# A three-layer graph attention stack on one core: chunk 0's sums during the count stage, 40 count tiles, and the maxima of five chunks over four chunks of products

## The reference, cut to what matters

```
h = x @ W
s = h @ a_src ; d = h @ a_dst
e = leaky_relu(s[src] + d[dst], 0.2)
m = segment_max(e, dst)
ex = exp(e - m[dst])
z = segment_sum(ex, dst)
out = segment_sum((ex / z[dst])[:, None] * h[src], dst) + b
```

## Time and profile before

| | |
|---|---|
| median of 3 runs | 714.85 us (714.55 to 715.75) |
| profiled execution | 714.44 us, its span 712.6 us |
| VectorE busy | 674.7 us (95%) |
| TensorE busy, its weight loads | 604.9 us (85%), 588.5 us (83%) |
| ScalarE busy | 463.8 us (65%) |
| GpSimd busy | 368.3 us (52%) |
| mean granted TensorE clock | 0.934 |
| chain that ended last | VectorE 56%, TensorE 30%, issue 9% |

### The profile page before, as it was taken

The page is one execution under the profiler, slowest core; times in us unless marked ns, Lnnn a source line. Parts: engine busy times, 40 slices in busy tenths (PEclk is TensorE's granted clock), DMA queues, the critical chain, the costliest instruction groups (busy, mean ns, idle before and its releaser), DMA issues.

```text
span 712.6 us, 13778 instructions
## 1 busy us (share of the span) xinstructions
PE 604.9 (85%) x5576; PEld 588.5 (83%) x5576; DVE 674.7 (95%) x939; ACT 463.8 (65%) x696; POOL 368.3 (52%) x354
## 2 busy tenths in 40 slices
PE   2657677675589899999999979999989889999995
PEld 1557666665589899999998979898979889999995
DVE  3999999999999999999999799999999989999995
ACT  0326666454497557575666768878776698687780
POOL 5581000000045454454675666758588677696883
PEclk9956889677789999999999999999999999999998
DMA  3410000001000000000100100000010010100001
GB/s 76 112 47 1 2 1 1 1 8 3 35 1 20 1 18 1 19 1 1 9 36 2 26 2 18 1 19 1 2 10 36 1 27 1 36 17 22 19 1 41
DMA packets 22325, 12.07 MB, mean 17 GB/s; under 512 B 12393, under 2 KB 20055, under 8 KB 22255
## 3 DMA queue, kind: packets, MB, share of 16 engines
q1 hardware_dynamic: 21455, 9.85, 5.9%
q0 software_dynamic: 800, 1.26, 0.6%
HBM read 9.47 MB, written 1.64 MB: 16 GB/s over the span
## 4 chain that ended last, share of the span: by engine, by line
DVE 56%; PE 30%; issue 9%; POOL 3%; ACT 1%; DMA 1%; DVEq 0%; POOLq 0%
PE ps L1739 23%; DVE scratch L864 22%; DVE ps L980 15%; DVE scratch L1062 9%; DVE ps L982 2%; DVE ps L992 2%; PE ps L1792 2%; PE ps L1695 1%; PE ps L1770 1%; POOL scratch L673 1%; DVE scratch L980 1%; DMA gathered<-in_edges,start_i 1%; DVE bn L814 1%; PE ps L1762 1%; PE ps L1795 0%
## 5 line engine op out<-in xcount | busy, mean ns | idle before, releaser
L1739 PE MATMUL ps<-hB,scratch 125*125 125x129 f32 x3450 | 404.2, 276 | 23.9 <-DVE scratch L1062 20.3
L1739 PEld LDWEIGHTS ps<-hB,scratch 125*125 125x125 f32 x3450 | 390.8, 189 | 32.2 <-DVE scratch L1062 24.5
L673 POOL TENSOR_TENSOR scratch<-scratch,C 125x625 f32<-125x625 f32 x197 | 250.8, 1284 | 178.9 <-ACT scratch L1500 178.9
L980 DVE SCALAR_TENSOR_TENSOR ps<-C,a_unit,ps 125x625 f32<-125x625 fp8e3 x330 | 278.0, 868 | 2.3
L1498 ACT ACTIVATE scratch<-gathered,r_neg 125x625 f32<-125x625 f32 x197 | 159.3, 809 | 43.1 <-PE ps L1739 40.9
L1500 ACT ACTIVATE scratch<-scratch,r_src 125x625 f32<-125x625 f32 x197 | 160.9, 817 | 6.4
L1062 DVE SCALAR_TENSOR_TENSOR scratch<-ps,r_src,C 125x625 f32<-125x625 f32 x178 | 153.5, 862 | 5.7 <-PE ps L1729 5.7
L1695 PE MATMUL ps<-scratch 128*128 128x125 bf16 x1250 | 105.9, 260 | 49.5 <-DVE scratch L864 49.5
L1695 PEld LDWEIGHTS ps<-scratch 128*128 128x128 bf16 x1250 | 99.8, 120 | 55.4 <-DVE scratch L864 54.1
L1363 ACT ACTIVATE C<-ps 125x1500 fp8e3<-125x1500 f32 (+2 forms) x60 | 75.3, 1270 | 73.8 <-PE ps L1695 73.5
L864 DVE TENSOR_TENSOR scratch<-key_lo,ps 128x5376 bf16<-128x5376 bf16 (+3 forms) x31 | 87.8, 2833 | 0.2 <-PE ps L1695 0.2
(11 more groups left out here) (185 smaller groups left out, 419.4 us busy)
## 6 DMA issues: line engine op xcount, KB each, us to landing
gathered<-g_lines SPq DMA_DIRECT2D x15, 305.2 KB
xr<-in_x SPq DMA_DIRECT2D x1, 1562.5 KB
out<-xr SPq DMA_DIRECT2D x4, 312.5 KB
edge_sb<-in_edges SPq DMA_DIRECT2D x1, 805.7 KB
gathered<-ext_lines SPq DMA_DIRECT2D x5, 122.1 KB
w<-in_W SPq DMA_DIRECT2D x2, 128.0 KB
out<-xr SPq DMA_DIRECT2D x1, 187.5 KB
out<-xr SPq DMA_DIRECT2D x1, 125.0 KB
```

The lines of the kernel that those rows point to most:

```text
L673: g.tensor_tensor(slot[s], slot[s], C5[:, q % NC, s, :], ALU.mult).then_inc(pool_done, 1)
L980: v.scalar_tensor_tensor(dest, counts, unit[:, s:s + 1], top, ALU.min, ALU.max).then_inc(S.top_done, 1)
L1739: last = mm(ps[0:P, acc_at(t):acc_at(t) + HW], A[:, P * t:P * (t + 1)], feat, start=opens and t in (0, 3), stop=closes, skip_group_check=True)
```

## The change

1. `SPLIT` cuts a chunk's windows into 8 tiles of up to 16, so there are 40 count tiles. This makes the one-hot buffers small enough that the ring of eight block buffers stands beside them in `scratch` (the ninth lies in `gathered`). The two halves of a tile are 8 and 8 windows.
2. The keys of chunks 1 to 4 are transposed at tiles 5 to 8, and the seven attention rounds stand at tiles 9 to 15. The extremes, scalars and exponentials follow at 16, 18 and 19.
3. All 25 blocks of chunk 0 are made by ScalarE and GpSimd within the count tiles 21 to 39 (`EARLY`), one or two a tile, and TensorE adds them two tiles later (`LAG`). GpSimd also scales the first layer's features (`scale_tiles`, five instructions of 645 columns, in place of 25 on ScalarE).
4. VectorE has no chunk 0 any more. Behind the first five maxima it goes on with the chunks of products 1 to 4, and the maxima of chunks 0 to 4 are spread over them (`FIRST_TOPS`). In chunks 1, 2 and 3 VectorE makes 5, 11 and 9 products (`OWN`); ScalarE and GpSimd make 20, 14 and 16. Chunk 4 and all later ones are as before.
5. What turns sums into the next features (`FIRST_LAYER`) stands later in chunks 1 to 3, in part in the chunk behind.

```diff
@@ -48,10 +48,10 @@
     assert EX % U == 0 and WC == P
-    SPLIT = (0, 21, 42, 63, 84, 105, P)
+    SPLIT = (0, 16, 32, 48, 64, 80, 96, 112, P)
...
     NT = NC * JT
-    WMAX = 21
+    WMAX = 16
@@ -178,9 +178,10 @@
-        ring = [scratch[0:P, i * CD:(i + 1) * CD] for i in range(RING + 1)]
+        ring = [scratch[0:P, 2 * OH + i * CD:2 * OH + (i + 1) * CD] for i in range(RING)]
+        ring.append(gathered[:, :, :].rearrange("p g e -> p (g e)").bitcast(fp32)[:, 1500:1500 + CD])
         slot = [ring[s % RING if s < T - 1 else RING] for s in range(T)]
-        at = (RING + 1) * CD
+        at = 0
@@ -228,12 +229,12 @@
                 ps[0:P, NEW + 512:NEW + 512 + 2 * AW].rearrange("p (t f) -> p t f", f=AW)]
-        PREP, VEC, CNT, COV = 2560, 2048, 3584, 3648
-        DIF, KEYS0, KEYS_AT = 3072, (0, 512), (3584, 3584 + KC * P)
+        PREP, VEC, CNT, COV = 1024, 2048, 3584, 3648
+        DIF, KEYS0, KEYS_AT = 2560, (0, 512), (3584, 3584 + KC * P)
         G0T, AB0 = 3584, 3584 + 4 * P
-        HALF = [(0, 12, 0), (12, WMAX, 2048)]
+        HALF = [(0, 8, 1024), (8, WMAX, 2048)]
         LAST_AT = 3072
-        IOTA = 1536
+        IOTA = 3072
@@ -361,11 +362,15 @@
         FEATS = tuple((t, min(t + 4, T)) for t in range(0, T, 4))
-        FEAT_AT = (5, 7, 9, 11, 13, 15, 17)
         KEYS_TILE = 4
-        EXT_AT, OVER_AT, EXPS_AT = 20, 23, 24
-        SCALED_AT = 26
-        SCALED = tuple(range(2, 10)) + (0, 1) + tuple(range(10, T))
+        FEAT_AT = tuple(KEYS_TILE + WG + r for r in range(len(FEATS)))
+        EXT_AT = FEAT_AT[-1] + 1
+        OVER_AT = EXT_AT + 2
+        EXPS_AT = OVER_AT + 1
+        EARLY_AT = EXPS_AT + 2
+        LAG = 2
+        EARLY = {t: tuple(range((t - EARLY_AT) * T // (NT - EARLY_AT), (t + 1 - EARLY_AT) * T // (NT - EARLY_AT)))
+                 for t in range(EARLY_AT, NT)}
@@ -376,6 +381,10 @@
                    At(1, (3, 4, 5, 6), 6, (8, 9, 10), None, (14, 17, 20), (None,) * 3, (None,) * 3, None, None))
+        FIRST_LAYER = (None,
+                       At(14, (15, 15, 16, 16), 16, (17, 17, 18), None, (23,), (21, 23, 27), (23, 25, 29), 25, 27),
+                       At(10, (11, 11, 12, 12), 12, (13, 13, 14), None, (20,), (17, 20, 25), (19, 22, 27), 22, 24),
+                       At(4, (5, 5, 6, 6), 6, (7, 7, 8), None, (16,), (13, 16, 22), (15, 18, 24), 19, 21))
@@ -392,7 +401,20 @@
+        OWN = ((), (15, 17, 19, 21, 23), (1, 4, 6, 8, 10, 12, 14, 16, 18, 20, 22), (1, 4, 7, 10, 13, 16, 18, 20, 22))
+        def spread_tops(q, k0, k1, s0, s1):
+            return tuple((s0 + (k - k0) * (s1 - s0) // (k1 - k0), q, k) for k in range(k0, k1))
+        AFTER = T
+        FIRST_TOPS = (None,
+                      spread_tops(0, AHEAD, T, 0, 13) + spread_tops(1, 0, 10, 14, 25) + spread_tops(1, 10, 14, AFTER, AFTER),
+                      spread_tops(1, 14, T, 0, 10) + spread_tops(2, 0, 17, 10, 25) + spread_tops(2, 17, 21, AFTER, AFTER),
+                      spread_tops(2, 21, T, 0, 4) + spread_tops(3, 0, T, 4, 24) + spread_tops(4, 0, AHEAD, AFTER, AFTER))
         def pool_tiles(q):
+            if q < len(OWN):
+                return tuple(s for s in range(T) if s not in OWN[q])
@@ -404,12 +426,22 @@
             L = (q - 1) // NC
+            if q < len(FIRST_LAYER):
+                return FIRST_LAYER[q]
...
-        def in_odd(k):
+        def in_odd(k, q=None):
+            if q in (1, 2):
+                return k % 2 == 1 and not any(at_ == AFTER and (c, k) == (q, k_) for at_, c, k_ in FIRST_TOPS[q])
...
         LAST_ODD = max(k for k in range(T) if in_odd(k))
+        def tops_before_rows(q):
+            if q in (2, 3):
+                c, k = min((c, k) for at_, c, k in FIRST_TOPS[q - 1] if at_ == AFTER)
+                return c * (T + 1) + k
+            return q * (T + 1) if q > 1 else 0
@@ -703,8 +735,12 @@
                 t1 = t0 + CT
-                pool.wait_ge(exps_ready, EXPS[L, 0 if t0 < EARLY_TILES else t0])
-                pool.wait_ge(F.pe_done, (L * NC - 1) * T + t1)
+                pool.wait_ge(exps_ready, EXPS[L, 0 if L == 0 or t0 < EARLY_TILES else t0])
+                if L:
+                    pool.wait_ge(F.pe_done, (L * NC - 1) * T + t1)
+                else:
+                    pool.wait_ge(keys_sb, 2 * WG)
+                    pool.wait_ge(h_ones, 1)
@@ -748,12 +784,17 @@
                             scale_tiles(L, LATE)
-                    if q < NC and s in B2_AT:
+                    if q == 0 and s % CT == 0:
+                        scale_tiles(0, s)
+                    if 0 < q < NC and s in B2_AT:
...
                         block_product(q, s)
+                if q == 0:
+                    for t in range(CT):
+                        second_bias(t)
@@ -1075,12 +1123,15 @@
                     elif s == 0:
-                        dve.wait_ge(F.rows_ready, q + 1)
-                    for k in range(AHEAD, T):
-                        if top_at(q, k) == s:
-                            next_top(q, k)
-                    if s == join_at(q):
-                        join_tops(F, q)
+                        dve.wait_ge(F.rows_ready, q)
+                    if q < len(FIRST_TOPS):
+                        first_tops(q, s)
+                    else:
+                        for k in range(AHEAD, T):
+                            if top_at(q, k) == s:
+                                next_top(q, k)
+                        if s == join_at(q):
+                            join_tops(F, q)
@@ -1153,7 +1205,7 @@
                 next_top(0, k)
-            for q in range(Q):
+            for q in range(1, Q):
@@ -1499,17 +1531,39 @@
+            def count_stage():
+                for t in range(NT):
+                    if 0 < t - KEYS_TILE < WG:
+                        copy_keys(t - KEYS_TILE)
+                    if t + 1 in FEAT_AT:
+                        normalise_first(FEAT_AT.index(t + 1))
+                    if t in FEAT_AT:
+                        features_out(FEAT_AT.index(t))
+                    if t == EXPS_AT:
+                        act.wait_ge(sig_ready, 1)
+                        exps_dst(0, 0, T)
+                        exps_src(0, 0, T)
+                        first_negative_r()
+                    counts_out(t, 0)
+                    if t in FEAT_AT:
+                        attention_out(FEAT_AT.index(t))
+                    for p in EARLY.get(t, ())[:1]:
+                        row_maximum(0, p)
+                    counts_out(t, 1)
+                    for p in EARLY.get(t, ())[1:]:
+                        row_maximum(0, p)
...
                 for s in range(T):
-                    if q == 0 and s + 10 < T:
-                        scale_features(SCALED[s + 10])
...
                         after_sums(F, q - 1, post_at(q), s)
+                    if 1 < q <= len(FIRST_LAYER):
+                        after_sums(F, q - 2, post_at(q - 1), s + T)
@@ -1529,15 +1583,13 @@
+            count_stage()
...
             act.wait_ge(half_out[1], NT + 1)
-            for s in SCALED[8:10]:
-                scale_features(s)
-            act.wait_ge(rneg_ready, 1)
-            for p in POOL_OF[0]:
-                if pass_at(0, p) < 0:
-                    row_maximum(0, p)
-            for q in range(Q):
+            for p in POOL_OF[1]:
+                if pass_at(1, p) < T:
+                    row_maximum(1, p)
+            for q in range(1, Q):
@@ -1721,11 +1759,11 @@
                     pe.wait_ge(g_done, LINES[L, EARLY_TILES])
-                if q:
+                if q > 1:
...
                 for t in range(CT):
-                    if t == CT - 1 and q:
-                        pe.wait_ge(F.top_done, q * (T + 1))
+                    if t == CT - 1 and q > 1:
+                        pe.wait_ge(F.top_done, tops_before_rows(q))
@@ -1806,6 +1844,31 @@
+            def first_block(s):
+                pe.wait_ge(pool_done, s + 1)
+                if s % CT == 0:
+                    pe.wait_ge(y_scaled, s // CT + 1)
+                if s < T - 2:
+                    products(slot[s], hB3[:, s, :], F.pe_done, s == 0, False)
+                elif s == T - 1:
+                    last_products(0)
+            def count_stage():
+                pe.wait_ge(keys_sb, 2)
+                for t in range(NT):
+                    if t == KEYS_TILE:
+                        sum_covered()
+                    if 0 < t - KEYS_TILE < WG:
+                        transpose_keys(t - KEYS_TILE)
+                    if t in FEAT_AT:
+                        features(FEAT_AT.index(t))
+                    count(t, t == NT - 1)
+                    for s in EARLY.get(t - LAG, ()):
+                        first_block(s)
+                for t in range(NT - LAG, NT):
+                    for s in EARLY[t]:
+                        first_block(s)
@@ -1813,10 +1876,8 @@
                         pe.wait_ge(prod_done, prod_no(q, s) + 1)
-                    if q == 0:
```

(5 more changed lines are left out.)

75 lines of the change are left out of this document (27 added, 48 removed).

## The result

The changed kernel took 710.65 us (median of four, 708.67 to 712.06) beside 715.11 for the kernel before: ratio 0.9935, 95% interval 0.991 to 0.9961. The gain is 4.5 us; the forecast had 11.2. The profiled execution was the fastest of the four, 708.67 us with a span of 706.9, which is 5.7 less than the span of before. So part of the miss lies in the profile (5.5 us: 708.67 for 703.2) and part in the distance from it to the median (2.0 us, where 0.4 was allowed).

The account below looks back on a forecast made before the run. VectorE bounds the count stage; TensorE, with VectorE 1.2 us behind, the first layer's steady chunk. Z to chunk 5 shrinks 17.0 us, less 5.8 for Z moving: 11.2 off 714.44 is 703.2, plus 0.4 gives 703.6 us, range 692.5 to 712.

Parts of the forecast that it names:

- Z: Start of the first maximum, after the count stage: 198.35 us in before, forecast to move by 5.8 us.
- (b)1: Hand-over after Z: rows wait for chunk 0's last two blocks, arriving at Z+10.7; VectorE idles 6.3 us.
- (b)3: Chunk 1: transposes follow TensorE's block 14, so VectorE idles 5.7 us before L1033 and ends at Z+49.4.
- (b)2: Start of chunk 1: ScalarE makes six row blocks before copying sums; TensorE starts at Z+16.3, losing 1.7 us to its clock.
- (b)4: Chunks 2 and 3: VectorE binds with 43 big instructions each, 37.0 and 36.2 us; TensorE needs 34.2 at most.
- (b)5: Chunk 4: its 0.82 us of idle time goes, 35.5 becomes 34.7 us; chunk 5 starts at Z+157.3.
- (a)3: Attention rounds on tiles 9 to 15: chain of 5.1 to 6.7 us against VectorE's 4.4; stall 2 to 8, taken 3.
- (a)1: Count stage: 40 tiles for 30 give 20 more compare instructions at 0.06 us each, +1.2 us.
- (a)2: Count stage: node statistics, now behind four smaller tiles, wait for x to land, +0.8 us.
- (a)4: Count tiles from 21: 25 blocks on 19 tiles fit under 4.4 us on average; +0.8 us, bounds 0 and 3.
- ScalarE and TensorE pace the early blocks: Rival, count stage: rounds at half clock add 5 us, early tiles at mean clock 0.77 add 2.2: 711, chance 0.12.
- The product work wasn't the limit: Rival, first layer's products: maxima, 125 as before, and stalls eat the whole gain: 714.9, chance 0.04.

Follow-up runs that it names:

- e1_after: The changed kernel run again with no edit, beside the kernel before: 711.08 us, ratio 0.9953.
- e9_rows: Changed kernel with TensorE's row broadcast for chunk 1 called ahead of the last products of chunk 0: 710.4 us, ratio 0.9946.
- e2_pool: Changed kernel with three products each of chunks 2 and 3 moved from VectorE to ScalarE and GpSimd: 705.97 us, ratio 0.9885.
- e12_terms: Changed kernel with attention products behind their tile's count products, and ScalarE's copy of their results behind its half 1 copy: 706.7 us, ratio 0.9874.
- e6_spread: Changed kernel with attention rounds on tiles 9, 10, 12, 13, 15, 16, 18 and early blocks from tile 24: 709.95 us, ratio 0.9927.
- e14_all: Changed kernel with e12_terms' order, e2_pool's products, and rows, sums copy, transposes and kappa exponential earlier around chunk 1: 700.71 us, ratio 0.9795.

## Why the prediction was right in sign and wrong in size

The miss is 7.0 us (710.65 for 703.6). On the forecast's own clock it is 1.0 before Z, -0.3 to the end of chunk 1, 4.6 in chunks 2 to 4, 0.2 behind, and 1.6 between the profile and the median. None of the three signs of being wrong that the prediction names came: the clock after tile 21 was 0.91, a 4096-element compare took 2.28 us, and ScalarE had copied half 0 of the last tile at Z+1.7 (forecast Z+2.6). Of what it says would show it, two things failed: chunk 5 came 161.6 us after Z and not some 157, and VectorE idled in chunk 3.

**What bounds the kernel, (b)1 to (b)3: right.** Both engines lost work, the rows, the first block and L1033 came within 1.1 us of their places. But e1_after and e9_rows show that VectorE's wait for the rows, which (b)1 lists, decides nothing; the path runs over ScalarE's six row blocks, its copy and TensorE's fifteen blocks, as (b)2 and (b)3 compute it.

**(b)4 and (b)5 are the steps that failed: chunks 2 to 4 were under-priced.** The forecast gave 37.0, 36.2 and 34.7, the profile has 37.6, 38.7 and 36.2: 4.6 us, the largest part of the miss. For chunk 3 the count left out three things. It joins two sets of maxima, chunk 2's and its own, as VectorE's timeline shows:

```profile
295.79 0.81 DVE L1027 TENSOR_TENSOR scratch<-scratch,ps 125x625 f32<-125x625 f32 x1
...
308.05 3.19 DVE L1021 SCALAR_TENSOR_TENSOR ps<-C,a_unit,ps 125x625 f32<-125x625 fp8e3 x4
...
325.23 0.81 DVE L1027 TENSOR_TENSOR scratch<-scratch,ps 125x625 f32<-125x625 f32 x1
...
326.98 3.60 DVE L1021 SCALAR_TENSOR_TENSOR ps<-C,a_unit,ps 125x625 f32<-125x625 fp8e3 x4
```

Each costs 0.72 to 0.84, and 0.9 for the maximum ahead of it. Second, it too waits for the transposes (0.80 at 300.76), which I charged to chunk 2 alone. Third, a maximum that follows one into the same accumulator, which the kernel makes wait for the former by a semaphore, starts 0.91 after it (the four at 326.98) and not 0.78 (the four at 308.05), and the small instructions behind L1033 take longer when they follow each other (0.93 from 300.76 to the one that reads its result; before, a product stood between them, 0.72 after it). By these rows the three make about 2.6 us, an estimate, of 2.5 missing. In chunk 4 I let the 0.82 us before the row broadcast vanish; it stayed to the hundredth, since TensorE, idle at times up to 347 us, is busy without a gap from there to 371 and ends the chunk. The other 0.7 of chunk 4 is one small instruction (L922), which took 0.88 us in place of 0.17; nothing in the trace says why. That VectorE binds chunks 2 and 3 was right (e2_pool), but not by the margin given: "TensorE needs 34.2 at most" left out the feature work that the change moves there, and TensorE was busy for 37.3 and 36.9 us.

**(a)3: the mechanism right, the size at the low end.** The forecast took 3 of 2 to 8 us, near the full clock, and the profile after has 2.9. The eleven profiles with this order of the rounds on tiles 9 to 15 run from 2.9 (clock 0.87) to 8.2 (0.70), and on the whole rise as the clock falls. The profile after was one of the best, so Z was only 1.0 late there, while the median is 2.0 above that execution, where the forecast added 0.4. That is the second part of the miss. The mean clock of the four executions falls as their time rises (0.958, 0.955, 0.954, 0.948), but only one of them has a trace, so in which stage the slower ones lost their time isn't shown. e12_terms shows the chain itself to be the cause of most of the stall, as (a)3 had it, and that it wasn't needed.

**(a)1, (a)2, (a)4: small errors that cancel.** 4096 and 4000 elements take 4.35 us a pair, 3328 and 3250 take 3.56; five times (7 x 4.35 + 3.56) less five times (5 x 5.66 + 5.40) is 1.6 (forecast 1.2). x cost 0.6 (0.8). The early blocks cost VectorE nothing from tile 21 on in the profile after (0.8). Just before Z VectorE waits 0.90 us for ScalarE's copy of counts, which the forecast doesn't have. In all VectorE has 3.1 us more work and 3.7 more idle time before Z. One microsecond of the work is an instruction of the set-up, which took 1.19 us in before (L842) and 2.20 after (L883). VectorE's row and GpSimd's, in before and then after:

```profile
47.56 1.19 DVE L842 TENSOR_TENSOR hB<-hB,gathered 125x1024 f32<-125x1024 f32 x1
...
44.13 2.39 POOL L624 TENSOR_TENSOR hB<-hB,gathered 125x1024 f32<-125x1024 f32 x1
```

```profile
43.01 2.20 DVE L883 TENSOR_TENSOR hB<-hB,gathered 125x1024 f32<-125x1024 f32 x1
...
44.08 3.36 POOL L656 TENSOR_TENSOR hB<-hB,gathered 125x1024 f32<-125x1024 f32 x1
```

In before GpSimd had ended (46.52) when VectorE began. With shorter tiles VectorE is there earlier, the two overlap, and both get longer by 1.0 us. So it is in all fifteen profiles with 40 tiles: 1.62 to 2.26 us on VectorE, 3.36 or 3.37 on GpSimd. GpSimd beside VectorE was priced at nothing from the compares, and for them that held.

**Rivals.** Half clock beside the early blocks and GpSimd against the compares (753, 742) are out: the clock from 106 to 205 us was 0.91, a 4096-element compare 2.28 us with GpSimd busy or idle. "ScalarE and TensorE pace the early blocks" (711) has the right number by coincidence: in the profile the rounds cost 2.9 us and not the 8 that it asks for, the early tiles nothing, and most of the miss lies in chunks 2 to 4, where it has none. "The product work wasn't the limit" is out too: six products less gained 4.2 us in chunks 2 and 3 (e2_pool). The time lies outside the forecast's own 699 to 708.5, though inside the outer range. One slip in the working: the bounds of Z's terms add up to 4 to 13 us, not 2 to 15.

## What to carry to other kernels

Count the instructions of each stage from the new order, joins and repeated waits too, where a steady stage's remainder is carried over: here 39 became 43 but the remainder grew as well, and so did TensorE's work, by 21 products a chunk. When two waits of one engine add up to the same in several executions, the first is probably not on the path; look at what ends the second, and test it by moving the first (e9_rows). On an engine that runs in order, put products that wait for another engine behind those that don't.

## What the runs showed of the hardware

Kernels whose code is the same in that stretch were granted a mean TensorE clock of 0.70 to 0.89 over the 46 us from 60 to 106 (0.87 and 0.89 in the two profiles of the changed kernel itself), and the same six products after the same 3.42 us wait ran in 0.90 or in 1.62 us. What decides between them none of these runs shows. The kernel's own times lie 2.3 us apart before the change and 5.5 after it; that the clock in this stretch does it is a guess, since e6_spread kept its stalls and narrowed to 2.3 while e14_all lost half of them and stayed at 5.2.

A VectorE maximum that waits by a semaphore for the one just before it, whose accumulator it reads, starts 0.90 us after it; into the other accumulator it is 0.78.

Two element-by-element instructions with both inputs in SBUF, one on VectorE and one on GpSimd, seem to take turns where they overlap. VectorE's, begun at 43.01, ends at 45.21, 1.09 us after GpSimd's former one (41.73, 2.39 long), and alone it takes 1.19; GpSimd's next ends 2.23 us after that, and alone it takes 2.39. In all fifteen profiles VectorE's ends 1.12 or 1.13 us after GpSimd's next one is said to start. The compares, which read one operand from PSUM, take 2.28 us for 4096 elements beside GpSimd's blocks and without them.
